# Wide attention on Trainium2: where the routing of the sparse stage is woven in, and in what pieces

## The reference, cut to what matters

```
x = x + tanh(g_xattn[1]) * _L1_xattn_ref(_layernorm(x), ctx, ctx, ...)   # 16 heads of 64, inner width 1024, output layernorm
x = x + tanh(g_ffn[1])   * _L1_ffn_ref(_layernorm(x), gate_w, gate_up_w, down_w)
# _L1_ffn_ref:
router_logits = x_flat @ gate_w                  # 8 experts
router_probs  = softmax(router_logits)
top_k_probs, top_k_idx = top_k(router_probs, 2)  # renormalised
hidden = silu(gate_out) * up_out; expert_out = hidden @ down_w
output = sum over the two picked experts of their rows times their shares
```

## Time and profile before

| | us |
|---|---|
| median of 3 runs | 1565.92 (1562.4 to 1566.38) |
| the profiled execution, its own time | 1570.91 |
| its span, first to last instruction | 1569.1 |
| busy: PE, DVE, ACT, POOL | 1293.9, 948.7, 722.1, 532.2 |
| granted clock of PE, mean | 0.896 |
| exponentials of the wide attention, first and last | 318.1, 556.8 |
| last DVE instruction of the stage, first of the next | 580.16, 584.24 |

### The profile page before, as it was taken

The page is one execution under the profiler, slowest core; times in us unless marked ns, Lnnn a source line. Parts: engine busy times, 40 slices in busy tenths (PEclk is TensorE's granted clock), DMA queues, the critical chain, the costliest instruction groups (busy, mean ns, idle before and its releaser), DMA issues. The chain is left out here.

```text
span 1569.1 us, 25219 instructions
## 1 busy us (share of the span) xinstructions
PE 1293.9 (82%) x8930; PEld 751.1 (48%) x8930; DVE 948.7 (60%) x2159; ACT 722.1 (46%) x1938; POOL 532.2 (34%) x625
## 2 busy tenths in 40 slices
PE   3799629879988859777996798989987978996998
PEld 2444317645555536454442455555654434442443
DVE  6466631355656754267564788878774865665664
ACT  3254413367756424343443565646664233453222
POOL 2320250545333252342001374747543320001443
PEclk8599859889999878895997899999988986998999
DMA  2455020240000011322000000000000001000000
GB/s 59 120 147 128 26 84 22 67 90 11 1 1 1 1 49 57 94 62 34 10 3 1 1 1 1 2 1 1 1 1 1 1 12 21 10 3 1 7 7 14
DMA packets 67134, 45.31 MB, mean 29 GB/s; under 512 B 17707, under 2 KB 60403, under 8 KB 67011
## 3 DMA queue, kind: packets, MB, share of 16 engines
q1 hardware_dynamic: 61155, 34.48, 8.5%
q0 software_dynamic: 4096, 8.40, 2.1%
q10 hardware_dynamic: 1760, 0.82, 0.3%
HBM read 24.91 MB, written 13.89 MB: 25 GB/s over the span
## 5 line engine op out<-in xcount | busy, mean ns | idle before, releaser
L3475 ACT ACTIVATE L2a_pr<-psum,L2a_negmax 128x512 f32<-128x512 f32 (+3 forms) x256 | 132.2, 531 | 94.2 <-DVE L2a_negmax L3601 40.2
L583 ACT ACTIVATE L1x_praw<-psum,L1x_negmax 128x154 f32<-128x154 f32 x256 | 96.2, 391 | 67.5 <-DVE L1x_negmax L708 67.4
L319 POOL TENSOR_TENSOR L1x_pm<-L1x_praw,L1x_total 128x1024 f32<-128x1024 f32 x32 | 60.7, 1898 | 144.6 <-DVE L1x_total L714 116.2
L3340 PE MATMUL psum<-ident,L2a_pr 128*128 128x128 f32 x640 | 85.9, 278 | 19.2 <-DVE L2a_pT L3614 11.8
L3340 PEld LDWEIGHTS psum<-ident,L2a_pr 128*128 128x128 f32 x640 | 71.7, 142 | 24.9 <-issue 21.2
L2042 POOL TENSOR_TENSOR L3f_scaled<-L3f_sg,L3f_wide 128x512 f32<-128x512 f32 (+1 forms) x44 | 55.8, 1272 | 66.8 <-ACT L3f_sg L2121 37.8
L1675 DVE TENSOR_REDUCE L3x_negmax<-psum 128x6 f32<-128x924 f32 (+1 forms) x48 | 47.7, 1012 | 46.7 <-PE psum L1213 37.4
L1675 DVE TENSOR_REDUCE L0x_negmax<-psum 128x6 f32<-128x924 f32 (+1 forms) x48 | 47.8, 1011 | 45.6 <-PE psum L1213 41.0
L3228 POOL TENSOR_TENSOR L2a_pr<-L2a_pr,L2a_total 128x768 f32<-128x768 f32 x32 | 48.6, 1520 | 69.9 <-DVE L2a_total L3630 69.6
L3225 POOL TENSOR_TENSOR L2a_pr<-L2a_pr,L2a_total 128x1024 f32<-128x1024 f32 x29 | 56.5, 1947 | 46.3 <-DVE L2a_total L3630 46.2
L708 DVE TENSOR_REDUCE L1x_negmax<-psum 128x4 f32<-128x616 f32 x64 | 50.8, 794 | 35.2 <-PE psum L389 32.4
(11 more groups left out here) (744 smaller groups left out, 3363.9 us busy)
## 6 DMA issues: line engine op xcount, KB each, us to landing
expert_arena<-in_L_ffn_w SPq DMA_DIRECT2D x16, 256.0 KB, 4.5
group_in<-zero SPq DMA_DIRECT2D x2, 1472.0 KB, 9.3
L1f_xs<-group_in SPq DMA_DIRECT2D x10, 256.0 KB, 4.1
group_out<-L1f_ys SPq DMA_DIRECT2D x10, 256.0 KB, 2.3
L1f_gu<-in_L_ffn_gate_up_w SPq DMA_DIRECT2D x8, 256.0 KB, 3.8
slots_in<-zero SPq DMA_DIRECT2D x1, 1280.0 KB, 9.1
L0f_xs<-slots_in SPq DMA_DIRECT2D x5, 256.0 KB, 4.2
resid<-in_x SPq DMA_DIRECT2D x4, 256.0 KB, 5.8
```

The lines of the kernel that those rows point to most:

```text
L319: nc.gpsimd.tensor_tensor(pm[:, n % 2].rearrange("p j t k -> p (j t) k"), praw[:, n % 3, :, :, 0:MAIN].rearrange("p j t k -> p (j t) k"), ...
L583: nc.scalar.activation(praw[:, n % 3, j, t, :], psum[:, 2 * u + j, x * CTX:(x + 1) * CTX], ACT.Exp, bias=negmax[:, n % 2, u, j, x:x + 1], ...
L3340: last = nc.tensor.transpose(psum[:, TURN + n // 4, n % 4 * P:(n % 4 + 1) * P], pr[:, m % RING, n * P:(n + 1) * P], core.ident[:])
L3475: ins = nc.scalar.activation(pr[:, i % RING, SEQ * j + lo:SEQ * j + hi], psum[:, bank + j, lo:hi], ACT.Exp, bias=negmax[:, i % RING, e:e + ...
```

## The change

- The routing of group 0 uses bank IN instead of H0 and H1, and the turned rows of batch 0 go to `xnT` instead of `core.x1`. The three waits in front of `turned` go; PE waits for `lg` before `rows_back(2)` in unit 27, for `yr` before `ranks`, and for `rank` before the last `rows_back`.
- `spread` moves to unit 22, `spread_root` to 23, `front` of one batch each to 23 and 24, `rowsT` and `rows_out` to 24 and 25, `logits` and the first `best` to 26, the second `best` to 27, `ranks` and `place` to 28, `table` to 29.
- POOL scatters two row tiles (4 DMAs) after each of units 29, 30 and 31, and the last two after the loop.
- `finished(2, 1)` moves from unit 27 to 30, `finished(2, 2)` from 29 to iteration 32, `finished(2, 3)` from 30 to iteration 33; ACT's `root(2)` moves from unit 28 to behind the loop.

```
--- before.py
+++ after.py
@@ -278,7 +278,7 @@
         got = sb("got", [P, 2 * QT * D])
         flat = praw[:].rearrange("p a j t k -> p (a j t k)")
         rows = got[:].rearrange("p (b t d) -> p b t d", b=2, d=D)
-        turned_rows = [core.x1[:].rearrange("p n d -> p (n d)")[:, 0:SEQ], xn[:, 1].rearrange("p t d -> p (t d)")]
+        turned_rows = [xnT[:], xn[:, 1].rearrange("p t d -> p (t d)")]
         results = [flat[:, 0:2 * QT * D], flat[:, 2 * QT * D:4 * QT * D], got[:], got[:]]
 
         def key_unit(i):
@@ -327,9 +327,10 @@
                     ins.then_inc(s["nt"], 1)
                     if n == 12:
                         grouped.constants(nc.gpsimd)
-                    if n == NS - 2:
-                        grouped.scatter(nc.gpsimd, 0, rows.rearrange("p b t d -> p (b t) d"), 0, 2)
-                grouped.scatter(nc.gpsimd, 0, rows.rearrange("p b t d -> p (b t) d"), 2, 2 * QT)
+                    if n >= NS - 3:
+                        t0 = 2 * (n - NS + 3)
+                        grouped.scatter(nc.gpsimd, 0, rows.rearrange("p b t d -> p (b t) d"), t0, t0 + 2)
+                grouped.scatter(nc.gpsimd, 0, rows.rearrange("p b t d -> p (b t) d"), 6, 2 * QT)
 
             @block.tensor
             def _(pe):
@@ -493,16 +494,12 @@
                             pe.wait_ge(s["vw"], 4 * b + (5, 7).index(g) + 1)
                         if n < NS and b >= 2 and g in (1, 2):
                             pe.wait_ge(s["vw"], 4 * (b - 1) + 2 + g)
-                        if b == B - 1 and g == 3:
-                            pe.wait_ge(grouped.s["xt"], 2)
-                        if b == B - 1 and g == 4:
-                            pe.wait_ge(grouped.s["lg"], 1)
-                        if b == B - 1 and g == 6:
-                            pe.wait_ge(grouped.s["rank"], 1)
                         turned(m)
                     if b and b < B and g == 3:
                         if follows:
                             pe.wait_ge(s["q"], n + NG)
+                        else:
+                            pe.wait_ge(grouped.s["lg"], 1)
                         rows_back(b - 1)
                     if 0 < n < NS:
                         scores(n, 1)
@@ -515,21 +512,22 @@
                         if g == 0:
                             rowsT(b + 1, IN)
                         query(n + NG, IN)
-                    if n < NS and b == B - 1 and g in (2, 3, 5):
-                        pe.wait_ge(s["pt"], 2 * (n - 2) + 1)
-                        if g == 2:
-                            grouped.rowsT(pe, 0, rows[:, 0], H0)
-                        if g == 3:
-                            grouped.logits(pe, 0, turned_rows, H0)
-                        if g == 5:
-                            grouped.ranks(pe, 0, H0)
+                    if b == B - 1 and g == 0:
+                        pe.wait_ge(s["q"], NS)
+                        grouped.rowsT(pe, 0, rows[:, 0], IN)
+                    if b == B - 1 and g == 1:
+                        pe.wait_ge(grouped.s["xt"], 1)
+                        grouped.rowsT(pe, 1, rows[:, 1], IN)
+                    if b == B - 1 and g == 2:
+                        grouped.logits(pe, 0, turned_rows, IN)
+                    if b == B - 1 and g == 4:
+                        pe.wait_ge(s["yr"], B - 1)
+                        grouped.ranks(pe, 0, IN)
                     if n >= 3 and n % 2 and n - 2 < NS:
                         tails(n - 2)
                     if n < NS:
                         if n >= 2:
                             pe.wait_ge(s["pt"], 2 * (n - 2) + 2)
-                        if b == B - 1 and g == 2:
-                            grouped.rowsT(pe, 1, rows[:, 1], H1)
                         if follows and g in (2, 5, 7):
                             keys(b + 1, (2, 5, 7).index(g), H0)
                         if b and n % 2 and (follows and g in (3, 5) or b >= 2 and g == 1):
@@ -540,6 +538,7 @@
                             values_out(b + 1, g // 2 - 2, H0)
                         if b >= 2 and g in (0, 1):
                             values_out(b, 2 + g, H0)
+                pe.wait_ge(grouped.s["rank"], 1)
                 rows_back(B - 1)
                 grouped.experts(pe, 0)
 
@@ -635,7 +634,7 @@
 
                 for n in range(NS):
                     b, g = n // NG, n % NG
-                    if b == B - 1 and g == 1:
+                    if n == NS - NG - 1:
                         grouped.spread_root(act, 0)
                     if n:
                         exps(n, 0)
@@ -648,17 +647,17 @@
                             keys(b + 1, (2, 5, 7).index(g), H0)
                         if b and g in (2, 3, 5):
                             values_turned(b + 1, (2, 3, 5).index(g), H1)
-                    if b == B - 1 and g == 2:
-                        for x in range(2):
-                            grouped.rows_out(act, x, turned_rows[x], (H0, H1)[x])
+                    if b == B - 1 and g in (0, 1):
+                        grouped.rows_out(act, g, turned_rows[g], IN)
                     if n == 6:
                         rows_root(2)
                     if n == 14:
                         rows_root(3)
                     if b and g == 2:
                         output(b - 1)
-                    if b and g == 4:
+                    if b and b + 1 < B and g == 4:
                         root(b - 1)
+                root(B - 2)
                 output(B - 1)
                 root(B - 1)
 
@@ -784,13 +783,8 @@
                             values_out(b + 1, g // 2 - 2, H0)
                         if b >= 2 and g in (0, 1):
                             values_out(b, 2 + g, H0)
-                    if b and b < B and g >= 3:
-                        if g == 3:
-                            finished(b - 1, 1)
-                        if g == 5:
-                            finished(b - 1, 2)
-                        if g == 6:
-                            finished(b - 1, 3)
+                    if b and b + 1 < B and g in (3, 5, 6):
+                        finished(b - 1, (3, 5, 6).index(g) + 1)
                     if n == 2:
                         summed(2)
                     if n == 7:
@@ -799,18 +793,20 @@
                         summed(3)
                     if n == 15:
                         normed(3)
+                    if n == NS - NG - 2:
+                        grouped.spread(0)
+                    if n in (NS - NG - 1, NS - NG):
+                        x = n - NS + NG + 1
+                        grouped.front(dve, v, x, rows[:, x])
                     if b == B - 1:
-                        if g == 0:
-                            grouped.spread(0)
-                        if g == 1:
-                            for x in range(2):
-                                grouped.front(dve, v, x, rows[:, x])
-                        if g in (3, 4):
-                            grouped.best(dve, v, 0, g - 3, H0)
+                        if g in (2, 3):
+                            grouped.best(dve, v, 0, g - 2, IN)
+                        if g == 4:
+                            grouped.place(dve, v, 0, IN)
                         if g == 5:
-                            grouped.place(dve, v, 0, H0)
-                        if g == 6:
                             grouped.table(dve, v, 0)
+                    if n in (NS - 2, NS, NS + 1):
+                        finished(B - 2, (NS - 2, NS, NS + 1).index(n) + 1)
                 for part in range(4):
                     finished(B - 1, part)
 

```

## The result

| | before | changed |
|---|---|---|
| median, us | 1566.38 | 1554.91 (1552.59 to 1556.78, 5 runs) |
| ratio to before, 95% interval | | 0.9927, 0.9909 to 0.9945 |
| profiled execution, its own time | 1570.91 | 1555.14 |
| span | 1569.1 | 1553.1 |

One of the five runs of the kernel before took 4832.86 us and says nothing of the kernel; the other four lie between 1562.4 and 1568.03.

The account below looks back on a forecast made before the run. The path was taken as the chain from unit 23 to unit 31's `pm`, then to DVE's finish at 580.33. Terms -7.5 + 1.5 (clock) + 1.4 (POOL) + 0.3 (tail) = -4.3 us gave 1561.6 us, range 1557.0 to 1568.0.

Parts of the forecast that it names:

- POOL isn't last: Block's end: POOL's last scatter issue ends 1.0 us before DVE's finish at 580.33, so the finish chain sets the end.
- Units 22 to 26: Earlier fronts and logits: unit 24 starts 0.8 us later, 25 2.2 later, 26 0.4 earlier, 27 4.2 later.
- Units 27 to 29: Routing and finish work leave these units: units 28, 29 and 30 start 0.8, 1.2 and 7.5 us earlier.
- The clock (+1.5): PE's low clock on the path of the last batch's units costs 1.5 us, between ends of 0 and 5.7.
- my upper end of 2.85 us each: Most that PE groups of one unit at half clock were said to cost; two low stretches give 5.7 us.
- Scatter in pieces (+1.4): Four issues before each `pm`: 15.1 us from `pm` of 29 to `pm` of 31 instead of 13.7, loss 1.4.
- The tail (+0.3): From `pm` of 31 to DVE's end, 0.3 us added for a longer low clock while PE waits for POOL.
- the slower clock: Rival: low clock after logits and ranks falls on the path, +5.0 us, 1570.9 us; chance 0.14.
- POOL's dear issues: Rival: issues beside busy DVE take up to 1.61 us, eight before `pm` of 31, +0.9, 1566.8 us; chance 0.19.
- The better one: Rival: no low clock on the path, shorter low stretch over next stage's start, -8.4 us, 1557.5 us; chance 0.15.
- the signs: Checks named beforehand, among them no DVE idle over 2 us in iterations 32, 33 and block's end 4 to 5 us earlier.
- The pair of ACT's table loads: Two 1.28 us table loads around ACT's root go away; counted as nothing, 2.5 us better by the skill's switch price.

Follow-up runs that it names:

- E1: Kernel before with all 16 scatters after unit 31, none after unit 30; ratio to before 0.9993, stretch 101.03 us (before 101.19).
- E6: Kernel before with only the scatters in pieces, as in the changed kernel; ratio to before 0.9991, stretch 99.14 us.
- E12: Kernel before with eight chained memsets on POOL behind its last scatter; ratio to before 1.0027, stretch 103.21 us.
- E4: Changed kernel with scatters and batch 2's finish as before, so the routing's move alone; ratio to before 0.9958, stretch 94.15 us.
- E5: Kernel before with only batch 2's finish moved late and ACT's root behind the loop; ratio to before 0.9943, stretch 93.99 us.
- E8: Kernel before with 3 and 5 extra unread PE matmuls ahead of two waits, units 28 and 30; ratio to before 0.9983, stretch 99.30 us.
- E11: The changed kernel run again, nothing altered; ratio to before 0.9929, stretch 91.55 us (88.68 in the first profile).
- E10: Changed kernel with 6 of PE's 23 register loads moved ahead of unit 31's transposes; ratio to before 0.9926, stretch 88.65 us.
- E2: Changed kernel with POOL's old scatters, 4 after unit 30 and 12 after unit 31; ratio to before 0.995, stretch 91.69 us.
- E9: Changed kernel scattering one row tile after each of units 28 to 31 and four after the loop; median 1549.63 us, ratio to before 0.9889.
- E7: Kernel before with scatters in pieces and batch 2's finish late, routing where it was; ratio to before 0.9942, stretch 94.88 us.

## Why the prediction was wrong

The direction was right, and so was the largest term, the shorter units 27 to 29. The size was not: -12.5 in the stretch for -4.3. The step that failed is that POOL isn't last, and with it the clock's term; by its own steps:

- *Units 22 to 26.* Right. Unit 24 starts 0.7 us later (forecast 0.8), unit 25 1.8 later (2.2). Unit 26 starts 1.1 us earlier (forecast 0.4), and unit 27 3.2 later for 4.2 forecast. DVE's wait for the logits is there.
- *Units 27 to 29.* The mechanism is right, the size too small. Units 28, 29 and 30 start 2.5, 3.0 and 9.6 us earlier, where the hand sum had 0.8, 1.2 and 7.5. Of these 2.1 us, 1.2 are the low clock of the before profile in unit 28 (E1, E6, E12), which is luck of that execution. E4 and E5 add what the sum couldn't know: either the routing's move or the finish's alone brings 7 us.
- *The clock (+1.5).* Wrong. The changed kernel has no low stretch in units 26 to 31. And E8 shows that such a stretch lies off the path in units 29 and 30, and costs up to 1.65 us in unit 28. So my upper end of 2.85 us each (the sum of the three groups it lists, not of six) was a price of PE, not of the run.
- *Scatter in pieces (+1.4).* Right to 0.1: 15.09 us from `pm` of 29 to `pm` of 31.
- *The tail (+0.3).* It came out at -1.6 (17.3 instead of 18.9 from `pm` of 31 to DVE's end); E11's went the other way, 20.0. The place of the low stretch has its part: before, it fell on the values behind `pm` of 31, which took 3.42 us (the row stands at E11) and 1.88 in the changed kernel (552.94). Of the seven profiles with the routing moved five have 17.3 to 17.6 here (the others 18.5 and 20.0); of the seven without, none is under 18.4. So part of it may belong to the change; which part isn't shown. The finish of batch 2 in iterations 32 and 33 was covered, and part 3 ends 0.9 us before the next step of DVE.
- *"POOL issues its last scatter until 579.30, 1.0 us sooner, so it isn't last"*: this step failed outright, and is worth 2.7 us. I compared the ends of the instructions. But from POOL's last instruction to the next stage it takes 4.94 us, 4.0 of them its DRAIN, and from DVE's at most 1.21 (E1, E12, E10). Before, POOL was last by 2.7 us. The pieces, which I had booked as a loss only, took 8 instead of 12 issues behind unit 31 and made POOL's end cheap.

Together: 2.1 + 1.5 + 1.9 + 2.7 = 8.2 us missed. Of these 1.2 are the low clock of the before profile in unit 28 and so luck, and part of the tail's 1.9 may be. Of the rivals, the slower clock and POOL's dear issues didn't come: issues took 0.95 to 1.05 us. The better one had the right sign and half of its reason: no low stretch lay on the path in units 26 to 31. The other half, a shorter low stretch over the next stage's start, is not seen: that start is at 1.2 GHz for 13.5 us, 14.1 before. Of the signs, two missed: DVE is idle 2.20 and 2.92 us in iterations 32 and 33, waiting for PE's transposes, where no more than 2 was expected, and the block ends 12.5 us sooner on the stretch's axis, not 4 to 5.

The pair of ACT's table loads (counted at nothing) did go; its worth stays open as a term of its own, since E5 has it together with the finish. The chance of 0.14 for slower was spent on a mechanism that wanted the clock on the path. A range built from the clock and POOL's issue time alone was too narrow, since it held no term for how a block ends.

## What to carry to other kernels

At the end of a stage ask each engine for its last instruction and for the step from there to the next stage. These steps differ, and an engine that looks 1 us early can be the last by 2.7. Look at the DRAIN of each engine there. The parts of a change need not add: with both in place a wait can come back that either one alone had covered, so price each with the others in place. And a low clock costs nothing where another engine sets the pace, so look for it on the path first.

## What the runs showed of the hardware

- From POOL's last instruction to the next stage's first DVE instruction: 4.93 to 4.96 us in the eight kernels in which POOL was last (before, E1, E2, E4, E5, E8, E9, E12), whether the last instruction was a DMA issue or a memset. From DVE's last: 1.20 to 1.21 us in the six profiles in which DVE was.
- POOL's DRAIN at this block's end is through 3.99 to 4.01 us behind its last instruction in all fourteen profiles. In the profile before it is 0.05 to 0.07 us at block ends without indirect DMAs, and 1.39 to 2.88 at those with 10 to 32.
- PE's low clock isn't the same from execution to execution of the same code: unit 28 lasted 6.66 us once and 5.41 to 5.46 three times, and from `pm` of 31 to DVE's end the changed kernel took 17.3 and 20.0 us.
- Eight scatters in a row behind `pm` of 31 took 0.95 to 1.02 us each in the changed kernel, partly beside DVE's finish; single ones took 1.28 to 1.41 in E2, E4, E5, E7 and E12.
